# Attention on one core: the narrow matmuls of two key tiles gathered into one burst per pair of tiles

## The chip, the cores and the metric

The kernel runs on one core of a Trainium2 chip. The metric is the device time of one execution in microseconds (us). The kernel before took 3467.74 us, the median of three runs (3467.65 to 3473.09).

## What is computed

The program runs two layers over x of 2 sequences x 2048 tokens x 512 features. The first layer (a state-space mixer and a feed-forward network, both conditioned) is not touched. The second layer is attention with 16 heads of width 32:

```python
h = _sln(hidden, w, ln_g, ln_b, Wg, bg, Wb, bb)
qkv = (h @ Wqkv.T + bqkv).reshape(B, N, num_heads, hd, 3)
...
energy = jnp.einsum('bhqd,bhkd->bhqk', q, k)
att = jax.nn.softmax(energy, axis=-1) / D ** 0.5
out = jnp.einsum('bhqk,bhkd->bhqd', att, v)
...
out = out @ Wp.T + bp
```

followed by the residual and a second conditioned layer norm. The change lies wholly in the three middle lines: scores, softmax, weighted sum of the values.

## The kernel before

The attention stage works in **blocks**: one block is 512 queries of one sequence for a group of 4 heads. There are 32 blocks (4 head groups x 2 sequences x 4 query chunks). A block walks over 16 **tiles** of 128 keys (`kt` in the code). The work of one tile is:

- **Scores** (PE, `score`, L1554): 4 matmuls, one for each head, of 97 rows x 128 columns against 512 queries, into one of 3 PSUM banks in turn (banks 0 to 2). The 97th row adds minus the row maximum of each query.
- **Exponentials** (ACT, L1650): one pass over each score bank into `probs`, of which there are 8 tiles. The bank is free again when the pass is done; `score` waits for the pass of three scores ago (`exp_ready`, L1551).
- **Value matmuls** (PE, `weigh`, L1565): 4 matmuls in fp32, one for each head, each 32 columns wide, side by side in bank 6 (the trace shows each as 2 instructions, so 8 in a group). They come `AV_LAG` = 2 tiles after the scores of the tile.
- **Ones matmuls** (PE, `total`, L1575): 4 matmuls of the same narrow form with a matrix of ones, for the softmax denominators, into bank 7. They take the sum of the probabilities of two tiles (`pair`, added by POOL, L1711) and come at odd tiles, `SUM_LAG` = 5 tiles late.

The kernel subtracts the true row maximum, so it finds it one block ahead. For that PE makes the scores of the **following** block in the other orientation (`search`, L1540, 96 rows x 128 queries against 512 keys), into 3 PSUM banks of their own in turn (banks 3 to 5), and DVE reduces each to a column of maxima (`find`, L1673). A block has 64 searches, spread over its tiles by `SHARES` (L1402): 4 in tile 0, 5 in each of tiles 1 to 12, none in tiles 13 to 15. A search waits until DVE has read the bank of three searches ago:

```python
pe.wait_ge(max_read, MAXES * (NB * it + n) + max(j - 2, 0))
```

When the 64 maxima are there, DVE turns and negates them, SP copies them into the row of the queries of the next block, and DVE divides the block before by its denominators (L1681, L1685).

Each engine works through its own instructions in the order in which the program lists them. The order on PE is written out in `one` (L1589): per tile score 0, search, score 1, search, then the narrow matmuls, then search, score 2, search, score 3, search. `searches()` issues nothing once the share of the tile is used up. Blocks 0 and 31 stand by themselves; the others run in a loop of four blocks a turn (`blocks`, L1432), with the same order.

Of the kernel before, what the change touches and what calls it, by code (L numbers as in the profile page):

```python
# [1380 lines left out]
def attention_stage(nc, sb, sem, psum, a, wp, first, q_dram, k_dram, v_dram, att_dram):  # L1381
# [21 lines left out]
    AV_LAG, SUM_LAG = 2, 5  # L1403
# [28 lines left out]
    def blocks(engine, block):  # L1432

        block(0, 0, True, False)
        with engine.Fori(0, ITERS - 1) as it:
            for n in range(1, NB):
                block(it, n, False, False)
            block(it + 1, 0, False, False)
        for n in range(1, NB):
            block(ITERS - 1, n, False, n == NB - 1)  # L1440

    with nc.Block() as block:
# [86 lines left out]
        @block.tensor  # L1529
        def _(pe):  # L1530
            def search(it, n, j):

                kc, qt, h = j // (HG * TT), j // HG % TT, j % HG
                if j == 0:
                    pe.wait_ge(q_ld[n], (Q_LD + ROW_LD) * it + Q_LD)
                if j in (0, MAXES // 2):
                    pe.wait_ge(k_ld[n // PB][2 * j // MAXES], 48 * (it // PER_GROUP + 1))

                pe.wait_ge(max_read, MAXES * (NB * it + n) + max(j - 2, 0))
                nc.tensor.matmul(psum[:, MX + j % 3, :], queries[n][0:R, h, qt * P:(qt + 1) * P],  # L1540
                                 keys[n // PB][0:R, h, kc * CH:(kc + 1) * CH], start=True, stop=True).then_inc(max_ready, 1)

            def score(it, n, kt, h):

                if kt == 0 and h == 0:

                    pe.wait_ge(q_ld[n], (Q_LD + ROW_LD) * (it + 1))
                unit = UNITS * n + HG * kt + h

                if unit >= 3:  # L1550
                    pe.wait_ge(exp_ready, NB * UNITS * it + unit - 2)  # L1551
                elif not (n == 0 and isinstance(it, int)):
                    pe.wait_ge(exp_ready, NB * UNITS * it)
                nc.tensor.matmul(psum[:, SC + unit % 3, :], keys[n // PB][0:R + 1, h, kt * P:(kt + 1) * P], queries[n][0:R + 1, h, :],  # L1554
                                 start=True, stop=True).then_inc(sc_ready, 1)

            def weigh(it, n, kt):

                tile = NKT * (NB * it + n) + kt
                pe.wait_ge(exp_ready, HG * (tile + 1))  # L1560
                if kt == 0:
                    pe.wait_ge(o_copied, NB * it + n + 1)
                    pe.wait_ge(v_ld[n // PB], 16 * (it // PER_GROUP + 1))
                for h in range(HG):
                    mm = nc.tensor.matmul(psum[h * HD:(h + 1) * HD, OUT, :], values[n // PB][:, kt, h * HD:(h + 1) * HD], probs[kt % NPROB][:, h, :],  # L1565
                                          start=(kt == 0), stop=(kt == NKT - 1))
                mm.then_inc(av_ready, 1)

            def total(it, n, p):

                pe.wait_ge(pair_ready, PAIRS * (NB * it + n) + p + 1)
                if p == 0:
                    pe.wait_ge(den_copied, NB * it + n + 1)
                for h in range(HG):
                    mm = nc.tensor.matmul(psum[h * HD:(h + 1) * HD, DEN, :], ones[:, :], pair[p % 2][:, h, :],  # L1575
                                          start=(p == 0), stop=(p == PAIRS - 1))
                mm.then_inc(sums_ready, 1)

            def lagged(it, n, kt, lag):

                if kt >= lag:
                    return it, n, kt - lag
                return (it, n - 1, kt + NKT - lag) if n > 0 else (it - 1, NB - 1, kt + NKT - lag)

            def pair_of(it, n, kt):

                return it, n, kt // 2

            def one(it, n, first, last):  # L1589
                following = (it, n + 1) if n < NB - 1 else (it + 1, 0)  # L1590
                j = iter(() if last else range(MAXES))
                for kt in range(NKT):

                    share = [next(j, None) for _ in range(SHARES[kt])]

                    def searches():
                        if share and (at := share.pop(0)) is not None:
                            search(*following, at)

                    if first and kt == AV_LAG:  # L1600
                        pe.wait_ge(consts, 1)
                        pe.wait_ge(ones_ld, 16 * (B - 1))
                    score(it, n, kt, 0)
                    searches()
                    score(it, n, kt, 1)
                    searches()
                    if kt >= AV_LAG or not first:
                        weigh(*lagged(it, n, kt, AV_LAG))
                    if (kt - SUM_LAG) % 2 == 0 and (kt >= SUM_LAG or not first):
                        total(*pair_of(*lagged(it, n, kt, SUM_LAG)))  # L1610
                    searches()
                    score(it, n, kt, 2)
                    searches()
                    score(it, n, kt, 3)
                    searches()

            blocks(pe, one)
            for kt in range(NKT, NKT + AV_LAG):
                weigh(ITERS - 1, NB - 1, kt - AV_LAG)
            for kt in range(NKT + 1, NKT + SUM_LAG, 2):  # L1620
                total(ITERS - 1, NB - 1, (kt - SUM_LAG) // 2)
# [381 lines left out]
```

## Time and profile before

| | us |
|---|---|
| median of three runs | 3467.74 |
| time of the profiled execution | 3469.48 |
| its span, first to last instruction | 3467.7 |
| attention stage in the span, about | 1440 to 3305 |
| mean granted TensorE clock, share of full | 0.967 |

The span is the part of the execution from the first to the last recorded instruction. PE stands for the matmul engine and PEld for its weight loads; DVE, ACT, POOL and SP are the vector, scalar, GpSimd and sync engines. A time in brackets in a timeline row is the idle time of the engine before that row, with what ended it. In a timeline, instructions that follow each other without a gap are merged into one row with a count. PE's durations overlap: the start of the next matmul says how long one occupies the array, not its own duration.

### The profile page before, as it was taken

The numbers are of one execution on the slowest core, as the hardware profiler recorded it, in microseconds if no ns is written. First come the engines' busy times: TensorE is split into PE (matmuls) and PEld (weight loads), VectorE is DVE, ScalarE is ACT, GpSimd is POOL, SyncE is SP. The second block draws the span as 40 slices with busy tenths as digits, with TensorE's granted clock in tenths as the row PEclk, the third lists the DMA queues.
The fourth block names the chain that finished last, engine by engine and source line by source line (L and its number), as shares of the span: only waits on it lengthen the run. The fifth ranks groups of instructions, "written<-read, shape, count | busy, mean of one in ns | idle before, by whom it ended". The sixth has DMA issues, their size and how long they took to land. (4 is left out here: it accounts for less than half of the span.)

```text
span 3467.7 us, 52215 instructions
## 1 busy us (share of the span) xinstructions
PE 3200.3 (92%) x16326; PEld 1973.9 (57%) x16326; DVE 2216.4 (64%) x3513; ACT 1527.7 (44%) x2770; POOL 1566.3 (45%) x538
## 2 busy tenths in 40 slices
PE   4786999999997989899999999999999999999976
PEld 2675777787775767644444444444444444444354
DVE  7885222222214436478888788888787887888458
ACT  2222232322222322355555555555555555556632
POOL 2665211001111110166666666666666665666655
PEclk8887999999998999999999999999999999999988
DMA  6233100000002463511031201122101230100044
GB/s 245 77 110 115 49 22 4 23 24 24 25 13 103 167 191 131 157 27 26 14 74 32 56 14 25 32 56 62 26 13 26 62 74 14 26 13 7 4 162 147
DMA packets 119434, 214.40 MB, mean 62 GB/s; under 512 B 11719, under 2 KB 29147, under 8 KB 118794
## 3 DMA queue, kind: packets, MB, share of 16 engines
q1 hardware_dynamic: 119180, 211.20, 20.3%
q8 instruction: 136, 2.23, 0.3%
q14 instruction: 118, 0.97, 0.1%
HBM read 135.34 MB, written 75.53 MB: 61 GB/s over the span
## 5 line engine op out<-in xcount | busy, mean ns | idle before, releaser
L1711 POOL TENSOR_TENSOR pair<-probs 128x2048 f32<-128x2048 f32 x256 | 1173.3, 4583 | 739.4 <-ACT probs L1650 739.4
L1673 DVE TENSOR_REDUCE part_max<-psum 128x1 f32<-128x512 f32 x1984 | 1227.7, 682 | 334.9 <-PE psum L1540 334.4
L1650 ACT ACTIVATE probs<-psum 128x512 f32<-128x512 f32 x2048 | 1068.6, 602 | 764.5 <-PE psum L1554 763.9
L1540 PE MATMUL psum<-keys,queries 96*128 96x512 f32 x1984 | 833.6, 420 | 5.2 <-DMA queries<-q_parts 5.2
L1554 PE MATMUL psum<-queries,keys 97*128 97x512 f32 x2048 | 794.1, 409 | 40.4 <-ACT probs L1650 28.9
L1540 PEld LDWEIGHTS psum<-keys,queries 96*128 96x128 f32 x1984 | 375.1, 189 | 458.8 <-DVE part_max L1673 375.2
L1565 PE MATMUL psum<-probs,values 128*32 128x512 f32 x4096 | 547.0, 606 | 4.1 <-ACT o_sum L1632 2.9
L1554 PEld LDWEIGHTS psum<-queries,keys 97*128 97x128 f32 x2048 | 381.1, 190 | 245.0 <-ACT probs L1650 176.9
L980 DVE TENSOR_TENSOR h_lo<-w_stage,h_hi 128x512 fp32r<-128x512 f32 x128 | 96.7, 756 | 528.3 <-ACT h_hi L918 528.3
L911 ACT ACTIVATE w_stage<-psum,b_col 128x512 f32<-128x512 f32 x128 | 88.3, 690 | 510.0 <-PE psum L38 510.0
L1024 POOL TENSOR_TENSOR ffn_u_lo<-ffn_u,ffn_u_hi 128x512 fp32r<-128x512 f32 x32 | 41.2, 1287 | 553.9 <-DVE ffn_u_hi L970 553.9
L1575 PE MATMUL psum<-pair,att_ones 128*32 128x512 f32 x2048 | 266.6, 592 | 2.7 <-POOL pair L1711 2.7
L36 PE MATMUL psum<-ffn_u_hi,w_hi 128*128 128x512 f32 x512 | 204.0, 398 | 6.4 <-DVE b_parts L1006 6.4
L36 PE MATMUL psum<-w_hi,h_hi 128*128 128x512 f32 x512 | 203.4, 397 | 0.0
L38 PE MATMUL psum<-ffn_u_lo,w_hi 128*128 128x512 f32 x512 | 203.0, 396 | 0.0
L37 PE MATMUL psum<-ffn_u_hi,w_lo 128*128 128x512 f32 x512 | 202.9, 396 | 0.0
L37 PE MATMUL psum<-w_hi,h_lo 128*128 128x512 f32 x512 | 202.8, 396 | 0.0
L38 PE MATMUL psum<-w_lo,h_hi 128*128 128x512 f32 x512 | 202.2, 395 | 0.0
L1565 PEld LDWEIGHTS psum<-probs,values 128*32 128x32 f32 x4096 | 80.9, 108 | 139.7 <-issue 97.2
L1371 POOL TENSOR_TENSOR qkv_u_lo<-qkv_u,qkv_u_hi 128x512 fp32r<-128x512 f32 x32 | 41.2, 1288 | 263.7 <-DVE qkv_u_hi L1316 263.7
L1575 PEld LDWEIGHTS psum<-pair,att_ones 128*32 128x32 f32 x2048 | 66.5, 110 | 156.2 <-issue 150.4
L1681 DVE RECIPROCAL den<-den 128x512 f32<-128x512 f32 x32 | 106.9, 3341 | 48.4 <-ACT den L1637 48.4
(305 smaller groups left out, 3734.9 us busy)
## 6 DMA issues: line engine op xcount, KB each, us to landing
queries<-q_parts SPq DMA_DIRECT2D x96, 256.0 KB, 4.8
keys<-k_parts SPq DMA_DIRECT2D x42, 512.0 KB, 7.2
x<-in_x_dram SPq DMA_DIRECT2D x8, 1024.0 KB, 7.9
y<-in_x_dram SPq DMA_DIRECT2D x8, 1024.0 KB, 6.4
y_rows<-y SPq DMA_DIRECT2D x8, 1024.0 KB, 5.1
qkv_z<-z_rows SPq DMA_DIRECT2D x8, 1024.0 KB, 5.5
q_parts<-qk_hi SPq DMA_DIRECT2D x32, 256.0 KB, 2.0
q_parts<-qk_lo SPq DMA_DIRECT2D x32, 256.0 KB, 2.3
```

The lines of the kernel that those rows point to most:

```text
L36: nc.tensor.matmul(out, w_hi, x_hi, start=first, stop=False)
L37: nc.tensor.matmul(out, w_lo, x_hi, start=False, stop=False)
L38: return nc.tensor.matmul(out, w_hi, x_lo, start=False, stop=last)
L980: dve.tensor_tensor(h_lo[j % NH][:, :], g[j % 2], h_hi[j % NH][:, :].bitcast(F32), ALU.subtract).then_inc(glo_ready, 1)
L1540: nc.tensor.matmul(psum[:, MX + j % 3, :], queries[n][0:R, h, qt * P:(qt + 1) * P], keys[n // PB][0:R, h, kc * CH:(kc + 1) * CH], start=Tr ...
L1554: nc.tensor.matmul(psum[:, SC + unit % 3, :], keys[n // PB][0:R + 1, h, kt * P:(kt + 1) * P], queries[n][0:R + 1, h, :], start=True, stop= ...
L1565: mm = nc.tensor.matmul(psum[h * HD:(h + 1) * HD, OUT, :], values[n // PB][:, kt, h * HD:(h + 1) * HD], probs[kt % NPROB][:, h, :], start= ...
L1575: mm = nc.tensor.matmul(psum[h * HD:(h + 1) * HD, DEN, :], ones[:, :], pair[p % 2][:, h, :], start=(p == 0), stop=(p == PAIRS - 1))
L1650: act.activation(probs[kt % NPROB][:, h, :], psum[:, SC + unit % 3, :], ACT.Exp).then_inc(exp_ready, 1)
L1673: dve.tensor_reduce(part_max[:, at, kc:kc + 1], psum[:, MX + j % 3, :], AX.X, ALU.max).then_inc(max_read, 1)
L1681: dve.reciprocal(den[:, :], den[:, :]).then_inc(inverted, 1)
L1711: pool.tensor_tensor(pair[p % 2][:, :, :], probs[2 * p % NPROB][:, :, :], probs[(2 * p + 1) % NPROB][:, :, :], ALU.add).then_inc(pair_read ...
```

## The change

```diff
--- before.py
+++ after.py
@@ -1604,10 +1604,12 @@
                     searches()
                     score(it, n, kt, 1)
                     searches()
-                    if kt >= AV_LAG or not first:
-                        weigh(*lagged(it, n, kt, AV_LAG))
-                    if (kt - SUM_LAG) % 2 == 0 and (kt >= SUM_LAG or not first):
-                        total(*pair_of(*lagged(it, n, kt, SUM_LAG)))
+                    if kt % 2 == 1:
+                        for lag in (AV_LAG + 1, AV_LAG):
+                            if kt >= lag or not first:
+                                weigh(*lagged(it, n, kt, lag))
+                        if kt >= SUM_LAG or not first:
+                            total(*pair_of(*lagged(it, n, kt, SUM_LAG)))
                     searches()
                     score(it, n, kt, 2)
                     searches()
```

Value matmuls that stood in the even tile `kt` move to the odd tile `kt + 1`, ahead of the ones that stand there. They now come 3 tiles after their scores; those of odd tiles still come 2 after, and the ones matmuls stay where they were. No instruction is added or removed; the other engines keep their order and their waits.

Two places show it. The first is PE's order in block 0, tiles 6 and 7, both with five searches. Before, from the value matmuls of tile 4 (in the middle of tile 6) to the ones matmuls in the middle of tile 7:

```order
L1565 MATMUL psum<-probs4,values0 32x512 x4
L1540 MATMUL psum<-keys0,queries1 128x512
L1554 MATMUL psum<-queries0,keys0 128x512
L1540 MATMUL psum<-keys0,queries1 128x512
L1554 MATMUL psum<-queries0,keys0 128x512
L1540 MATMUL psum<-keys0,queries1 128x512
L1554 MATMUL psum<-queries0,keys0 128x512
L1540 MATMUL psum<-keys0,queries1 128x512
L1554 MATMUL psum<-queries0,keys0 128x512
L1540 MATMUL psum<-keys0,queries1 128x512
L1565 MATMUL psum<-probs5,values0 32x512 x4
L1575 MATMUL psum<-pair1,att_ones 32x512 x4
```

Now, over the same piece:

```order
L1540 MATMUL psum<-keys0,queries1 128x512 x2
L1554 MATMUL psum<-queries0,keys0 128x512
L1540 MATMUL psum<-keys0,queries1 128x512
L1554 MATMUL psum<-queries0,keys0 128x512
L1540 MATMUL psum<-keys0,queries1 128x512
L1554 MATMUL psum<-queries0,keys0 128x512
L1540 MATMUL psum<-keys0,queries1 128x512
L1554 MATMUL psum<-queries0,keys0 128x512
L1540 MATMUL psum<-keys0,queries1 128x512
L1565 MATMUL psum<-probs4,values0 32x512 x4
L1565 MATMUL psum<-probs5,values0 32x512 x4
L1575 MATMUL psum<-pair1,att_ones 32x512 x4
```

The value matmuls of tile 4 have gone down nine rows, to stand beside those of tile 5. Two searches meet where they stood, and 18 scores and searches (10 searches, 8 scores) now lie between two bursts.

The second place is PE's order in tiles 13 to 15 of a block, which hold no searches (names without buffer numbers; - before, + now):

```order
-L1565 MATMUL psum<-probs,values 32x512 x4
-L1575 MATMUL psum<-pair,att_ones 32x512 x4
-L1554 MATMUL psum<-queries,keys 128x512 x4
-L1565 MATMUL psum<-probs,values 32x512 x4
-L1554 MATMUL psum<-queries,keys 128x512 x4
-L1565 MATMUL psum<-probs,values 32x512 x4
+L1565 MATMUL psum<-probs,values 32x512 x8
+L1575 MATMUL psum<-pair,att_ones 32x512 x4
+L1554 MATMUL psum<-queries,keys 128x512 x8
+L1565 MATMUL psum<-probs,values 32x512 x8
 L1575 MATMUL psum<-pair,att_ones 32x512 x4
 L1554 MATMUL psum<-queries,keys 128x512 x2
```

Eight scores now run without a break, where four stood on each side of a group of value matmuls.

## Rows read from the trace of the kernel before

**Rows 1.** Page of the profile, part 1: busy us, share of the span, instructions.

```profile
PE 3200.3 (92%) x16326; PEld 1973.9 (57%) x16326; DVE 2216.4 (64%) x3513; ACT 1527.7 (44%) x2770; POOL 1566.3 (45%) x538
```

**Rows 2.** Windows: busy us (count) of PE, PEld, DVE, ACT, POOL; clock; DMA; GB/s.

```profile
1900.00:2300.00 400.00, 390.42 (x2196) 188.31 (x2196) 325.28 (x472) 234.47 (x454) 251.81 (x55) 1.00 0.16 37
3240.00:3300.00 60.00, 54.98 (x322) 18.19 (x314) 15.50 (x5) 39.84 (x77) 43.60 (x11) 1.00 0.03 10
```

**Rows 3.** Page, costliest groups: busy us, mean ns of one | idle before it, releaser.

```profile
L1673 DVE TENSOR_REDUCE part_max<-psum 128x1 f32<-128x512 f32 x1984 | 1227.7, 682 | 334.9 <-PE psum L1540 334.4
L1650 ACT ACTIVATE probs<-psum 128x512 f32<-128x512 f32 x2048 | 1068.6, 602 | 764.5 <-PE psum L1554 763.9
...
L1540 PEld LDWEIGHTS psum<-keys,queries 96*128 96x128 f32 x1984 | 375.1, 189 | 458.8 <-DVE part_max L1673 375.2
```

**Rows 4.** Timeline of PE, one tile pair with searches: start, duration (us), operation, count.

```profile
1920.63 1.04 PE L1575 MATMUL psum<-pair,att_ones 128*32 128x512 f32 x8
1921.60 0.50 PE L1540 MATMUL psum<-keys,queries 96*128 96x512 f32 x1
1921.94 0.40 PE L1554 MATMUL psum<-queries,keys 97*128 97x512 f32 x1
...
1923.60 0.40 PE L1540 MATMUL psum<-keys,queries 96*128 96x512 f32 x1
1923.93 1.07 PE L1565 MATMUL psum<-probs,values 128*32 128x512 f32 x8
1924.92 0.50 PE L1540 MATMUL psum<-keys,queries 96*128 96x512 f32 x1
...
1927.25 1.07 PE L1565 MATMUL psum<-probs,values 128*32 128x512 f32 x8
1928.13 1.04 PE L1575 MATMUL psum<-pair,att_ones 128*32 128x512 f32 x8
```

**Rows 5.** Timeline of DVE, the same tile pair.

```profile
1922.14 3.08 DVE L1673 TENSOR_REDUCE part_max<-psum 128x1 f32<-128x512 f32 x5 [1.10 <-PE psum L1540]
1925.46 3.08 DVE L1673 TENSOR_REDUCE part_max<-psum 128x1 f32<-128x512 f32 x5 [0.24 <-PE psum L1540]
```

**Rows 6.** Timeline of all engines: first and fifth search after a burst, and the maxima between.

```profile
1981.31 0.50 PE L1540 MATMUL psum<-keys,queries 96*128 96x512 f32 x1
...
1981.84 2.48 DVE L1673 TENSOR_REDUCE part_max<-psum 128x1 f32<-128x512 f32 x4 [1.08 <-PE psum L1540]
...
1983.29 0.40 PE L1540 MATMUL psum<-keys,queries 96*128 96x512 f32 x1
```

**Rows 7.** Timeline of all engines, tiles 13 and 14, which hold no searches.

```profile
1958.54 0.96 PE L1554 MATMUL psum<-queries,keys 97*128 97x512 f32 x3
1959.07 2.06 ACT L1650 ACTIVATE probs<-psum 128x512 f32<-128x512 f32 x4 [1.40 <-PE psum L1554]
...
1959.72 0.50 PE L1554 MATMUL psum<-queries,keys 97*128 97x512 f32 x1 [0.22 <-ACT probs L1650]
...
1960.15 1.07 PE L1565 MATMUL psum<-probs,values 128*32 128x512 f32 x8
```

**Rows 8.** Timeline of PE: the ones matmuls from tile 11 to tile 5 of the next block.

```profile
2010.25 1.04 PE L1575 MATMUL psum<-pair,att_ones 128*32 128x512 f32 x8
...
2017.27 1.04 PE L1575 MATMUL psum<-pair,att_ones 128*32 128x512 f32 x8
...
2023.36 1.04 PE L1575 MATMUL psum<-pair,att_ones 128*32 128x512 f32 x8
...
2030.15 1.04 PE L1575 MATMUL psum<-pair,att_ones 128*32 128x512 f32 x8
...
2037.76 1.04 PE L1575 MATMUL psum<-pair,att_ones 128*32 128x512 f32 x8
...
2045.23 1.04 PE L1575 MATMUL psum<-pair,att_ones 128*32 128x512 f32 x8
```

## The prediction

> **What bounds the kernel now.** I read four views in this order: the page's busy times, the attention stage by windows, the costliest groups, and the timelines of single tiles. The page gives PE 92% of the span [rows 1]. The change touches only the attention stage, and there PE is busy nearly all the time at a granted clock of 1.00, which is the 2.4 GHz level [rows 2]. A busy PE need not be what sets the pace, so I ask in the timeline which wait ends last.
>
> In tiles with searches PE does not pause. From one ones group to the next, at 1920.63 and 1928.13, lie 18 full-width matmuls (10 searches, 8 scores) and three narrow groups [rows 4]. The parts, from starts:
>
> - a score or search among its like: 1921.94 to 1923.60 is seven steps, 0.237 us each;
> - from the last search to a narrow group: 0.33 (1923.60 to 1923.93), so 0.09 more than that step;
> - a narrow group followed by another: 0.88 (1927.25 to 1928.13);
> - a narrow group followed by a search: 0.99 for a value group (1923.93 to 1924.92), 0.97 for the ones group (1920.63 to 1921.60), so about 0.1 more than 0.88;
> - from that search to the next score: 0.34, again 0.1 more than a step.
>
> So going into narrow matmuls and out again costs 0.09 + 0.10 + 0.10 = 0.29 us beside the work. A pair of tiles has two such bursts: 18 x 0.237 + 3 x 0.88 + 2 x 0.29 = 7.49, and the trace says 7.50.
>
> DVE is close behind. Five maxima take 3.08 us, one is 682 ns long, so they start (3.08 - 0.68) / 4 = 0.60 apart [rows 3, 5]. Ten need 6.0 of the 7.5 us. DVE idles 1.10 us after the burst of two groups and 0.24 after the single group [rows 5]. It never gets far behind, because a burst comes after every five searches and lets it catch up.
>
> What ties them is the ring of three search banks. After a burst at T (the first search, 1981.31) the first maximum starts at T + 0.53 (1981.84). The fifth search starts at 1983.29 = T + 1.98 [rows 6]. It needs the bank of the second, whose maximum ends at T + 0.53 + 0.60 + 0.68 = T + 1.81, and starts 0.17 later. So search k starts at no less than **T + 1.38 + 0.60 (k - 4)**. For k = 5 this is exactly where PE is anyway (0.34 + 7 x 0.237 = 2.00). Before the change every count starts anew after five searches. The weight loads of the searches already show 375.2 us idle that DVE ended, hidden under matmuls [rows 3].
>
> **The change, part by part.** It is only a move of value groups on PE; no DMA and no instruction of another queue moves.
>
> *Bursts saved.* One burst less in each of the 8 tile pairs of a block: -0.29 us a pair on PE.
>
> *Tiles with searches.* Now 10 searches stand between two bursts. By PE alone the tenth starts at 0.34 + 16 x 0.237 = T + 4.13. By the banks it starts at T + 1.38 + 6 x 0.60 = T + 4.98. The scores stand between the searches in PE's order, so they wait as well. The burst follows 0.33 later and lasts 0.88 + 0.88 + 0.97 = 2.73. The next T is at 4.98 + 0.33 + 2.73 = **8.04**, against 7.48: +0.56 us. Two value groups side by side are not in the rows; a value group ahead of the ones group is the nearest (0.88, taken), the value group ahead of a search the other end (0.99, kept for the range; nothing in the rows speaks for less than 0.88). During the burst DVE has two to three banks waiting, 1.3 us of work or so, then idles: 8.04 - 6.0 = 2.0 us a pair. Nothing gives that back, since only three searches can be ahead.
>
> Stretches from one ones group to the next, in a block (those of before in [rows 8]):
>
> - tiles 3 to 5, 5 to 7, 7 to 9, 9 to 11: four of ten searches, before 7.47 (2037.76 to 2045.23; 7.50 in rows 4), taken as 7.48. Now 8.04: 4 x 0.56 = +2.24.
> - tiles 1 to 3: before 7.61 (a short wait for the copy of the last sums stands in it, and goes, because the first value group now comes a tile later). Now 8.04: +0.43.
> - tiles 11 to 13: before 7.02. It has eight searches: the eighth at T + 3.78, two scores 0.48, then 0.33 + 2.73: 7.32. +0.30.
> - tiles 13 to 15: before 6.09, scores only. PE waits for ACT there: score 4 starts 1.18 after score 1, as the first exponential starts at + 0.53 and lasts 0.60; then 0.43 to the value group [rows 7]. Exponentials start (2.06 - 0.60) / 3 = 0.49 apart [rows 3, 7]. Now eight scores stand together, and score 8 needs exponential 5: 0.53 + 4 x 0.49 + 0.60 + 0.06 = 3.15. Then 0.43 + 2.73: 6.31. +0.22.
> - tiles 15 to 1 of the next block: before 6.79. Six searches and eight scores: banks allow search 6 at about T + 3.4 (first search at 0.8, ACT sets score 7 at 2.66 and score 8 at 3.15). Then 0.33 + 2.73: 6.47. -0.32.
>
> Sum 2.24 + 0.43 + 0.30 + 0.22 - 0.32 = +2.87 us a block. With 31 blocks that hold searches: +89.0. The last block has none, seven stretches x 0.22 = +1.5. Together **+90.5 us**. Costed at nothing: the row of maxima for the next block (SP's copy). The last maximum starts 0.53 + 7 x 0.60 = 4.7 after tile 11's burst, the next block's first score now at 7.32 + 6.31 + 0.6 = 14.2, so 9.5 us cover it; before it was about 5.0 against 13.7, 8.7 us. SP's reload of the values waits for the last value group of a block, tile 15's, which stays in its tile. ACT's `probs` are 8 tiles deep and the moved groups come 3 late instead of 2. The sum that POOL makes for a pair is wanted two pairs later as before. If one of these covers failed, it would be a wait once a block, not in every pair.
>
> The sum stands on the profiled execution, 3469.48, giving 3560.0; that is 1.7 above the median of the runs, so the median goes to **3558**.
>
> The Trainium skill, "TensorEngine Tiling (Array Packing)", section "Tiling Modes", says that changing the tiling mode drains the engine. Rows 4 agree, with 0.29 us for a change there and back. By this rule alone the change is a gain, the first rival below; the rule says nothing of the banks.
>
> **The rivals.**
>
> *PE stays the bound, faster.* Then only the saved bursts count: 8 x 0.29 x 32 = -74 us, 3394. For it: PE's 92%, DVE's 1.3 us idle in each pair. It needs the maxima at most (4.13 - 1.38) / 6 = 0.46 us apart; even to break even they would have to be 0.51. Against it: 0.60 in every row of five. A second way to it would be that the searches' wait lets scores pass, but PE keeps its order. Chance 0.06.
>
> *The two cancel.* Within 0.2%, 7 us, what a measurement of this kernel can tell from no change: needs a pitch near 0.51. Chance 0.02.
>
> *The forecast.* Slower by 90, between 57 and 124. If the hand-over after a maximum costs nothing (0.17 less): -0.85 us a block; if in addition the stretch 15 to 1 gains 0.2 more, -33 in all, 3525 with rounding. If two value groups take 0.99: 0.11 x 8 x 32 = +28; with 6 us more for maxima 0.61 apart, 3592. Chance 0.84.
>
> *DVE's own 0.68 sets the pitch,* not 0.60: the tenth search then starts 6 x 0.08 = 0.5 later, 5 stretches x 0.5 x 31 = +75 more, 3633. Against it: the merged rows of five. Chance 0.04.
>
> *The clock falls.* PE, now waiting some tenths of a us before each search, drops from 2.4 to 1.2 GHz at times. The 7.19 us of PE work in a pair would then take 14.4, 6.3 above 8.04; in one pair in ten (20 of 200) this is +130, 3690. Against it: the tiles without searches at 3240 to 3300 hold a wait in every tile, and the clock there is 1.00 [rows 2, 7]. Chance 0.04. The Trainium skill, "TensorE: Matmul & The Clock Gate", section "A second HAM failure mode: psum-queue depth-cycling", tells of such short idle gaps between matmul groups making the clock swing; by those windows this trace does not bear it out.
>
> **How the numbers follow.** The time is that of the forecast, 3558, its range 3525 to 3592, which holds 0.84 of the chance, less a little for terms I have not seen. Faster 0.06, same 0.02, slower 0.84 + 0.04 + 0.04 = 0.92.
>
> **What would show it.** In the profile after: ones groups 8.0 us apart in tiles 3 to 11 (7.2 if the rival holds); maxima in merged rows of about ten, 6.1 us long, then 2 us idle; PE idle before searches 6 to 10, released by DVE's maxima, some 0.1 to 0.2 us each; three narrow groups 0.88 apart; clock still 1.00 in the stage; tiles 13 to 15 at 6.3. The prediction is wrong if the tenth search stands near T + 4.1, if the pitch of the maxima moves off 0.60 when ten come in a row, or if PE finds another way to lose or save time inside the burst.

## The result, and the profile after

The changed kernel takes 3569.73 us (median of four runs, 3566.45 to 3574.98); the kernel before took 3468.75 in the runs beside it. The ratio is 1.0282, 95% interval 1.0269 to 1.0296: slower by about 100 us. The forecast was slower, 3558, in a range of 3525 to 3592.

The page after, part 1 and three of the costliest groups (busy us, mean ns of one | idle before it, releaser):

```profile
PE 3292.8 (92%) x16326; PEld 1959.2 (55%) x16326; DVE 2211.6 (62%) x3513; ACT 1566.1 (44%) x2770; POOL 1564.3 (44%) x538
...
L1675 DVE TENSOR_REDUCE part_max<-psum 128x1 f32<-128x512 f32 x1984 | 1208.3, 680 | 435.5 <-PE psum L1540 434.8
L1652 ACT ACTIVATE probs<-psum 128x512 f32<-128x512 f32 x2048 | 1107.2, 607 | 827.7 <-PE psum L1554 821.6
...
L1540 PEld LDWEIGHTS psum<-keys,queries 96*128 96x128 f32 x1984 | 373.0, 188 | 509.6 <-DVE part_max L1675 317.8
```

PE is as busy as before, 92% [rows 1], in a program 100 us longer, and one maximum of DVE (680 ns) and one exponential of ACT (607 ns) take what they took [rows 3]. None of these shares tells what happened. The weight loads of the searches idled 375.2 us until DVE before, 317.8 after: even this sum fell.

The timeline of PE over one ten-search stretch of the changed kernel does tell (start, duration; the row at 2012.11 holds the fifth and sixth search):

```profile
2009.16 1.04 PE L1575 MATMUL psum<-pair,att_ones 128*32 128x512 f32 x8
2010.13 0.50 PE L1540 MATMUL psum<-keys,queries 96*128 96x512 f32 x1
...
2012.11 1.00 PE L1540 MATMUL psum<-keys,queries 96*128 96x512 f32 x2
2012.94 0.40 PE L1554 MATMUL psum<-queries,keys 97*128 97x512 f32 x1
2013.20 0.50 PE L1540 MATMUL psum<-keys,queries 96*128 96x512 f32 x1
...
2014.40 0.50 PE L1540 MATMUL psum<-keys,queries 96*128 96x512 f32 x1
...
2014.99 0.50 PE L1540 MATMUL psum<-keys,queries 96*128 96x512 f32 x1
2015.43 1.92 PE L1565 MATMUL psum<-probs,values 128*32 128x512 f32 x16
2017.17 1.04 PE L1575 MATMUL psum<-pair,att_ones 128*32 128x512 f32 x8
2018.14 0.50 PE L1540 MATMUL psum<-keys,queries 96*128 96x512 f32 x1
```

From one ones group (2009.16) to the next (2017.17) it is 8.01 us; before it was 7.50 [rows 4]. From the sixth search on, each stands 0.60 after the last (2013.20, then 2014.40 two later, 2014.99), not two steps of 0.237, and each has a row of 0.50 us, like the first search behind a burst, against 0.40 in the flow. PE's rows show no pause before them; the wait stands in the rows of their weight loads (PEld), which idle 0.30 us until DVE before each of the last four searches:

```profile
2014.40 0.19 PEld L1540 LDWEIGHTS psum<-keys,queries 96*128 96x128 f32 x1 [0.30 <-DVE part_max L1675]
...
2014.99 0.19 PEld L1540 LDWEIGHTS psum<-keys,queries 96*128 96x128 f32 x1 [0.30 <-DVE part_max L1675]
```

The two value groups take 1.74 together, 0.87 each. The row of the tenth search is at T + 4.86, the value groups at T + 5.30; the forecast had 5.31.

DVE over the same time (start, duration, count, idle before):

```profile
2010.66 6.07 DVE L1675 TENSOR_REDUCE part_max<-psum 128x1 f32<-128x512 f32 x10 [1.94 <-PE psum L1540]
2018.67 6.07 DVE L1675 TENSOR_REDUCE part_max<-psum 128x1 f32<-128x512 f32 x10 [1.94 <-PE psum L1540]
```

Ten maxima run without a gap in 6.07 us, (6.07 - 0.68) / 9 = 0.60 apart, and then DVE idles 1.94 us while the burst runs; before it was twice 3.08 with 1.10 and 0.24 idle [rows 5].

Where the 100 us lie, from the starts of all 256 ones groups in both traces, summed over the 31 blocks with searches (the first ones group of block 0 stands in tile 5, so tiles 1 to 5 count 30 blocks):

```
stretch (tile to tile)     before   after   difference over the blocks
3-5, 5-7, 7-9, 9-11          7.48    8.01   +65.3 (four stretches)
1-3                          7.61    8.01   +10.3
11-13                        7.01    7.28    +8.4
13-15                        6.08    6.29   +19.1, of it 12.7 in 8 blocks at 7.8 to 7.9
15-1 of the next             6.79    6.52    -4.9
last block                                   +2.8, of it 1.5 in tiles 1 to 3, 8.25 instead of 6.68
sum                                        +100.9
```

The before and after columns are medians; the parts are rounded. In the last block's tiles 1 to 3 of the changed kernel the clock fell too (granted 0.59 over the value groups); 1.5 is its excess over the 6.78 that stand there in runs where it did not fall. One row holds something that was not in the forecast's main line: eight blocks spend 7.8 to 7.9 us in tiles 13 to 15 instead of 6.29. Two such stretches in PE's timeline, the slow one:

```profile
2049.45 0.96 PE L1554 MATMUL psum<-queries,keys 97*128 97x512 f32 x3
2050.64 2.45 PE L1554 MATMUL psum<-queries,keys 97*128 97x512 f32 x5 [0.23 <-ACT probs L1652]
2053.02 3.60 PE L1565 MATMUL psum<-probs,values 128*32 128x512 f32 x16
2056.37 1.13 PE L1575 MATMUL psum<-pair,att_ones 128*32 128x512 f32 x8
```

and a usual one:

```profile
2172.06 1.04 PE L1575 MATMUL psum<-pair,att_ones 128*32 128x512 f32 x8
2173.03 0.96 PE L1554 MATMUL psum<-queries,keys 97*128 97x512 f32 x3
2174.21 2.46 PE L1554 MATMUL psum<-queries,keys 97*128 97x512 f32 x5 [0.23 <-ACT probs L1652]
2176.60 1.92 PE L1565 MATMUL psum<-probs,values 128*32 128x512 f32 x16
2178.34 1.04 PE L1575 MATMUL psum<-pair,att_ones 128*32 128x512 f32 x8
```

In both the eight scores go alike. The two value groups, 1.74 us in the usual one, take 3.35 in the other. The windows (busy us of PE, PEld, DVE, ACT, POOL, then the granted clock):

```profile
2001.14:2009.16 8.02, 7.93 (x47) 3.69 (x43) 6.07 (x10) 4.85 (x9) 4.57 (x1) 1.00 0.00 0
2049.45:2053.02 3.57, 3.34 (x12) 1.42 (x8) 3.44 (x2) 3.03 (x7) 1.87 (x1) 1.00 0.02 2
2053.02:2056.37 3.35, 3.35 (x17) 0.81 (x20) 3.23 (x1) 1.00 (x3) 2.67 (x1) 0.52 0.02 5
```

During the scores the clock is 1.00, during the value groups 0.52, that is 1.2 GHz almost throughout. In the ten-search stretch, the first row, it is 1.00.

The clock falls at one more kind of place, and does so before the change too: where the loop of four blocks turns, PE pauses 1 to 2 us in the stretch from tile 15 to tile 1. The kernel before, PE's timeline and a window:

```profile
2430.17 0.73 PE L1554 MATMUL psum<-queries,keys 97*128 97x512 f32 x2
2433.07 0.49 PE L1554 MATMUL psum<-queries,keys 97*128 97x512 f32 x1 [2.17 <-issue]
...
2434.06:2437.47 3.41, 3.41 (x13) 1.08 (x12) 1.51 (x3) 0.88 (x2) 2.35 (x1) 0.50 0.78 187
```

Of the six turns, two fall to 0.50 behind the pause in this trace and take 10.5 to 10.7 us; the other four take 8.6 to 9.0. In the changed kernel it is two of six as well (10.5 and 10.8), so the 100 us hold nothing of it. In the runs below it is two to six of six, and this moves totals by several us.

### The profile page after: what moved, and what is told of

The parts are those of the page before. It is cut to its first block and busy times, and to the rows that moved or that the text cites. A ratio compares the mean times of both kernels' runs of the same rounds, so it can differ in the third digit from the quotient of the medians.

```text
span 3567.9 us, 52215 instructions
## 1 busy us (share of the span) xinstructions
PE 3292.8 (92%) x16326; PEld 1959.2 (55%) x16326; DVE 2211.6 (62%) x3513; ACT 1566.1 (44%) x2770; POOL 1564.3 (44%) x538
## 5 line engine op out<-in xcount | busy, mean ns | idle before, releaser
L1675 DVE TENSOR_REDUCE part_max<-psum 128x1 f32<-128x512 f32 x1984 | 1208.3, 680 | 435.5 <-PE psum L1540 434.8
L1652 ACT ACTIVATE probs<-psum 128x512 f32<-128x512 f32 x2048 | 1107.2, 607 | 827.7 <-PE psum L1554 821.6
L1540 PE MATMUL psum<-keys,queries 96*128 96x512 f32 x1984 | 895.3, 454 | 23.0 <-DMA queries<-q_parts 5.4
L1554 PE MATMUL psum<-queries,keys 97*128 97x512 f32 x2048 | 816.5, 414 | 31.2 <-ACT probs L1652 25.8
L1540 PEld LDWEIGHTS psum<-keys,queries 96*128 96x128 f32 x1984 | 373.0, 188 | 509.6 <-DVE part_max L1675 317.8
L1565 PE MATMUL psum<-probs,values 128*32 128x512 f32 x4096 | 507.8, 614 | 0.0
L1565 PEld LDWEIGHTS psum<-probs,values 128*32 128x32 f32 x4096 | 108.6, 111 | 230.0 <-ACT probs L1652 116.8
```

The lines of the kernel that those rows point to most:

```text
L1652: act.activation(probs[kt % NPROB][:, h, :], psum[:, SC + unit % 3, :], ACT.Exp).then_inc(exp_ready, 1)
L1675: dve.tensor_reduce(part_max[:, at, kc:kc + 1], psum[:, MX + j % 3, :], AX.X, ALU.max).then_inc(max_read, 1)
```

## The experiments

The theory, here "bank theory": the loss comes from the ring of three search banks together with maxima 0.60 us apart, which hold the sixth and later searches of a stretch. The gain of the saved bursts is real and smaller. Rivals: the longer burst itself, the value groups coming a tile later, the clock.

**Make DVE faster, in both kernels.** The edit, in `find`:

```diff
-dve.tensor_reduce(part_max[:, at, kc:kc + 1], psum[:, MX + j % 3, :], AX.X, ALU.max)
+dve.tensor_reduce(part_max[:, at, kc:kc + 1], psum[:, MX + j % 3, 0:CH // 2], AX.X, ALU.max)
```

On the kernel before. 

> The kernel before, with each maximum taken over 256 of the 512 scores of its bank (it leaves out half of the keys in the row maxima). DVE's maxima should start about 0.35 us apart instead of 0.60. Bank theory: before the change PE sets the pace in tiles with searches and the fifth search is just not held, so nothing moves: ones groups 7.45 to 7.48 apart, 3465 to 3469 us. Rival (DVE already set the pace before): 7.2 or less apart and at least 40 us faster.

Measured: 3472.86 us, ratio 1.0007 (0.9996 to 1.0018), ones groups 7.48 apart. DVE did not set the pace before. The total lies 4 us over the expected range; in the trace the stretches with a loop turn hold 7 us more than before, and the clock fell at four of the six turns.

On the changed kernel. 

> The changed kernel, with each maximum over 256 of 512 scores (half of the keys left out of the row maxima). Bank theory: with maxima 0.35 apart the tenth search is no longer held, ones groups stand 7.19 apart in tiles 3 to 11, and the saved bursts show alone: about 3468 - 5 x 0.29 x 31 - tiles 11 to 1 0.5 x 31 = 3405 to 3415, some us more if the clock still falls in tiles 13 to 15. Rival (the loss comes from the burst itself, from the value groups coming later, or from the clock): it stays within 10 us of 3570.

Measured: 3425.08 us, ratio to before 0.9861 (0.9844 to 0.9879). PE's timeline of one stretch:

```profile
2018.42 0.39 PE L1540 MATMUL psum<-keys,queries 96*128 96x512 f32 x1
2018.74 1.92 PE L1565 MATMUL psum<-probs,values 128*32 128x512 f32 x16
2020.48 1.04 PE L1575 MATMUL psum<-pair,att_ones 128*32 128x512 f32 x8
2021.45 0.50 PE L1540 MATMUL psum<-keys,queries 96*128 96x512 f32 x1
...
2027.60 1.04 PE L1575 MATMUL psum<-pair,att_ones 128*32 128x512 f32 x8
```

The ones groups stand 7.12 apart, the tenth search is followed at once by the burst. The weight loads of the searches, from the page of this kernel:

```profile
L1540 PEld LDWEIGHTS psum<-keys,queries 96*128 96x128 f32 x1984 | 378.6, 191 | 234.9 <-issue 156.2
```

The wait for DVE is no longer what ends most of their idle time. So the same edit that gives nothing before gives 145 us after: the loss hangs on the pace of DVE's maxima, and the change without it would be a gain of 44 us. A saved burst is worth 7.48 - 7.13 = 0.35 us, rather more than the 0.29 forecast. The rest to the expected 3405 to 3415 is mostly the clock: eight blocks stand at 7.9 in tiles 13 to 15 in this kernel too, as does one stretch of the last block, and it fell at five of the six loop turns. One maximum takes 424 ns. Where DVE has the next bank waiting, maxima start 0.34 to 0.36 apart, as expected; that is so for about a fifth of them, and most of the others start 0.46 to 0.48 apart, as PE now sends the searches.

**An eighth less.** The same edit with 448 columns, on the changed kernel. 

> The changed kernel with each maximum over 448 of the 512 scores (an eighth of the keys left out of the row maxima). From 680 ns at 512 and 424 ns at 256 one maximum should take 0.62, and they should start 0.54 apart. Bank theory: tenth search at 0.53 + 6 x 0.54 + 0.62 + 0.17 = T + 4.56, ones groups 7.5 to 7.6 apart in tiles 3 to 11, tiles 11 to 13 about 7.0, all other stretches as in the changed kernel: 3570 - 31 x 2.7 = 3486. Rival (a threshold, or something beside DVE holds the searches): 7.1 or 8.0 apart.

Measured: 3485.90 us, ratio 1.0049 (1.0033 to 1.0064). Ones groups 7.54 apart, tiles 11 to 13 at 6.95, the others as in the changed kernel. DVE's timeline:

```profile
1991.35 5.41 DVE L1675 TENSOR_REDUCE part_max<-psum 128x1 f32<-128x448 f32 x10 [2.15 <-PE psum L1540]
```

Ten in 5.41 us with 616 ns for one: 0.53 apart. 512, 448 and 256 columns give 8.01, 7.54 and 7.13: no threshold in the middle, the stretch follows the pitch until PE's own order holds it.

**One search bank less.** The changed kernel:

```diff
-pe.wait_ge(max_read, MAXES * (NB * it + n) + max(j - 2, 0))
+pe.wait_ge(max_read, MAXES * (NB * it + n) + max(j - 1, 0))
-nc.tensor.matmul(psum[:, MX + j % 3, :], ...
+nc.tensor.matmul(psum[:, MX + j % 2, :], ...
-dve.tensor_reduce(..., psum[:, MX + j % 3, :], AX.X, ALU.max)
+dve.tensor_reduce(..., psum[:, MX + j % 2, :], AX.X, ALU.max)
```

> The changed kernel with two search banks instead of three, the score banks untouched. Bank theory: a search waits for the maximum of two before, which starts at the earliest 0.17 + 0.68 after that one, so maxima are some 0.64 to 0.66 apart and the tenth search stands near T + 5.8: ones groups 8.85 apart in tiles 3 to 11 (8.01 with three banks), tiles 13 to 15 unchanged at 6.29; 3570 + 31 x 5.3 = 3735. Rival (the ring is not what holds): below 3600.

Measured: 3754.19 us, ratio 1.0804 (1.0779 to 1.0829), ones groups 8.88 apart, tiles 13 to 15 at 6.29. DVE's timeline:

```profile
2090.96 6.43 DVE L1675 TENSOR_REDUCE part_max<-psum 128x1 f32<-128x512 f32 x10 [2.44 <-PE psum L1540]
```

Ten maxima now take 6.43, (6.43 - 0.68) / 9 = 0.64 apart. The ring sets the time, as expected. The total lies 19 us over the expected 3735: the clock fell in tiles 13 to 15 of six blocks and at all six loop turns, for which nothing had been put in.

**One search bank more, at the cost of a score bank.** Eight banks are all there are, so four search banks leave two for the scores; on the changed kernel and on the one before:

```diff
-SC, MX, OUT, DEN = 0, 3, 6, 7
+SC, MX, OUT, DEN = 0, 2, 6, 7
-... max(j - 2, 0))          MX + j % 3        unit - 2)       SC + unit % 3
+... max(j - 3, 0))          MX + j % 4        unit - 1)       SC + unit % 2
```

(Shortened: the wait and the bank of a search, then those of a score; DVE and ACT read the same banks.)

> The changed kernel with four search banks and two score banks instead of three and three. Bank theory: search k waits for the maximum of four before, so the tenth starts at T + 1.38 + 5 x 0.60 = 4.38 instead of 4.98, ones groups 7.4 to 7.5 apart in tiles 3 to 11 (8.01 in the changed kernel). Tiles 13 to 15 get slower with two score banks, 7.0 instead of 6.3. In all 3570 - 5 x 0.6 x 31 + 0.7 x 39 = about 3505. Rival (burst or lag): tiles 3 to 11 stay at 8.0, the whole at 3590 or more.

> Control for the run before: the kernel before with four search banks and two score banks. Bank theory: PE sets the pace in tiles with searches, so a fourth search bank gives nothing there, 7.47 apart; two score banks cost in tiles 13 to 15 only, about 0.3 to 0.5 a pair: 3475 to 3490. Rival (search banks already bound before): 7.3 or less apart in tiles 3 to 11.

Measured: 3662.67 us on the changed kernel (ratio 1.0554, 1.0534 to 1.0574) and 3626.41 on the one before (1.0442, 1.0423 to 1.0461). Both expectations of the totals miss. In tiles 3 to 11 the changed kernel goes from 8.01 to 7.68, less than expected; the control goes from 7.48 to 7.99. What I left out is that a ring of two scores binds in tiles with searches too. The control's timeline, scores and exponentials behind a burst:

```profile
2052.34 0.40 PE L1554 MATMUL psum<-queries,keys 97*128 97x512 f32 x1
...
2052.77 2.27 ACT L1650 ACTIVATE probs<-psum 128x512 f32<-128x512 f32 x4 [2.15 <-PE psum L1554]
2052.81 0.40 PE L1554 MATMUL psum<-queries,keys 97*128 97x512 f32 x1
...
2053.42 0.50 PE L1554 MATMUL psum<-queries,keys 97*128 97x512 f32 x1
```

The third score starts at 2053.42, when the first exponential (2052.77, 0.60 long) is over, and so it goes on in every stretch. In the changed kernel the wait for DVE is gone (0.8 us in all in its table of waits, against 317.8 with three banks) and the wait of the scores for ACT has taken its place (483.7). The pair of runs fits the bank theory but is no clean test of it, since two rings change at once; it does show that no bank can be spared for the searches. In the changed kernel with two score banks, tiles 13 to 15 lie over 8 us in 28 of 31 blocks, and in each of the 28 the granted clock fell to 1.2 GHz around the value groups.

**The rivals' own parts.** The value groups together, but the ones group on its own in even tiles:

```diff
                     if kt % 2 == 1:
                         for lag in (AV_LAG + 1, AV_LAG):
                             ...
-                        if kt >= SUM_LAG or not first:
-                            total(...)
+                    elif kt >= SUM_LAG or not first:
+                        total(...)
```

with `SUM_LAG` 4 instead of 5 (and the ones groups behind the last block a tile earlier to match). 

> The value groups of two tiles stand together in odd tiles as in the change, but the ones group stands alone in even tiles (four tiles late). Bank theory: five searches between bursts again, the longest burst is two groups as before, and the number of bursts is that of before, so ones groups 7.48 apart and 3460 to 3472 us. Rival (value groups of even tiles coming three tiles late, or two of them side by side, cost): over 3500.

Measured: 3469.99 us, ratio 1.0001 (0.9991 to 1.0010). A value burst of two groups (x16) and a ones group in turn, PE's timeline:

```profile
1996.30 1.92 PE L1565 MATMUL psum<-probs,values 128*32 128x512 f32 x16
...
2000.48 1.06 PE L1575 MATMUL psum<-pair,att_ones 128*32 128x512 f32 x8
...
2007.95 1.06 PE L1575 MATMUL psum<-pair,att_ones 128*32 128x512 f32 x8
```

7.47 apart, as before the change. Value groups side by side and a tile late cost nothing; what costs is ten searches in a row.

The price of a burst, from the other side: the kernel before with the ones group one score and two searches further down:

```diff
                         weigh(*lagged(it, n, kt, AV_LAG))
+                    searches()
+                    score(it, n, kt, 2)
+                    searches()
                     if (kt - SUM_LAG) % 2 == 0 and (kt >= SUM_LAG or not first):
                         total(*pair_of(*lagged(it, n, kt, SUM_LAG)))
-                    searches()
-                    score(it, n, kt, 2)
-                    searches()
                     score(it, n, kt, 3)
```

> The kernel before with the ones group moved away from the value group, behind the next search, score 2 and search, so that odd tiles hold two bursts of one group. It prices a burst: PE pays 0.29 more in each pair of tiles, ones groups 7.77 apart, 8 x 32 x 0.29 = 74 us more, 3542. Rival (going in and out of narrow matmuls is hidden or cheap while others wait): 3500 or less.

Measured: 3531.77 us, ratio 1.0179 (1.0163 to 1.0194), 7.80 apart in tiles 3 to 11: 0.33 for a burst more. The total is 10 us under the expected one, because tiles 11 to 13 and 13 to 15 went down, 7.01 to 6.87 and 6.08 to 5.93, where 0.29 more had been expected. That was a hint for the last run.

**The tail of the block as before.** The changed kernel, but tiles 14 and 15 with a value group each:

```diff
+                    if kt in (14, 15):
+                        weigh(*lagged(it, n, kt, AV_LAG))
-                    if kt % 2 == 1:
+                    elif kt % 2 == 1:
...
```

(The ones matmuls keep their place in every odd tile.)

> The changed kernel, but tiles 14 and 15 keep one value group each as before. Expected: tiles 13 to 15 take 6.08 again instead of 6.29, and the half clock that the changed kernel shows there in eight blocks (7.8 to 7.9 instead of 6.29) is gone: 3570 - 31 x 0.2 - 14 = 3550. Rival (the clock falls for PE's waits before the searches, anywhere): rows at half clock stay, in other tiles, and the time is 3560 or more.

Measured: 3560.83 us, ratio 1.0269 (1.0251 to 1.0287); the profiled execution has a span of 3553.5. Tiles 13 to 15 take 6.08 in every block, and none shows the half clock. The waits of the searches for DVE are as in the changed kernel (315.7 us). So the half clock in tiles 13 to 15 comes with eight scores in a row, not with the waits before the searches. The time of the runs moved by 9 us, not 20, and by its letter the rival holds as well: 3560 or more, and rows at half clock in other tiles. These rows are the loop turns, five of six at half clock against two in the changed kernel; the six turns take 5.9 us more than in the kernel before, in the changed kernel 0.3. They don't speak for the rival's cause: the kernel before falls there too, none falls in tiles 3 to 11, where the searches wait, and before each of the five falls PE pauses for 1.6 to 1.9 us. How many turns fall differs from kernel to kernel, with no rule that the runs show.

**The change where it gains only.** The kernel before, with the value group of tile 14 moved from tile 0 to tile 1:

```diff
-                    if kt >= AV_LAG or not first:
+                    if kt >= AV_LAG:
+                        weigh(*lagged(it, n, kt, AV_LAG))
+                    elif kt == 1 and not first:
+                        weigh(*lagged(it, n, kt, AV_LAG + 1))
                         weigh(*lagged(it, n, kt, AV_LAG))
```

> The kernel before, but with only the value group of tile 14 moved from tile 0 to tile 1 of the next block, where six searches lie between the bursts. Bank theory: this stretch is the one where the change gains, 6.52 instead of 6.79, with nothing lost elsewhere: 31 x 0.27 = 8 us faster than before, 3460. Rival (no stretch with more searches than five may lose its burst): same or slower than 3468.

Measured: 3466.50 us, ratio 0.9988 (0.9979 to 0.9997). PE's timeline of the stretch:

```profile
2022.59 1.04 PE L1575 MATMUL psum<-pair,att_ones 128*32 128x512 f32 x8
...
2027.04 0.40 PE L1540 MATMUL psum<-keys,queries 96*128 96x512 f32 x1
2027.37 1.92 PE L1565 MATMUL psum<-probs,values 128*32 128x512 f32 x16
2029.11 1.04 PE L1575 MATMUL psum<-pair,att_ones 128*32 128x512 f32 x8
```

6.52 instead of 6.79. So it is in 17 of the 31 stretches from tile 15 to tile 1; every fourth, seven in all, goes from 7.75 to 7.53, and the one into the last block, which has no searches, rises from 6.08 to 6.29. The six turns of the loop take 2.7 us more than before, with three at half clock instead of two; all other stretches are as before. The mechanism is as expected, the gain in the time is 4 us of the expected 8, with an interval that nearly touches none.

**The opposite of the change.** With it, in tiles 13 to 15 and the last block, the groups spread out:

```diff
+                    spread = kt >= 13 or (last and kt >= SUM_LAG - 1)
...
+                    if spread and kt % 2 == 0:
+                        score(it, n, kt, 2)
+                        weigh(*lagged(it, n, kt, AV_LAG))
+                        score(it, n, kt, 3)
+                        continue
...
+                    late = spread and (kt < 15 or last)
...
+                    if late:
+                        total(*pair_of(*lagged(it, n, kt, SUM_LAG)))
```

(`late` takes the ones group from its old place to the end of the tile.) 

> The opposite of the change where PE has no searches, and the change where it gains: the kernel before with the value group of tile 14 in tile 1 of the next block (as in the run on the edge alone), and in tiles 13 to 15 (and the last block) the three narrow groups of a pair spread out, two or three scores apart. By the same steps the burst is then short enough for three score banks to bridge: tiles 11 to 15 take 7.8 + 4.65 = 12.45 from ones group to ones group instead of 13.1, pairs of the last block 5.4 instead of 6.08, tiles 15 to 1 6.5 instead of 6.79, rest as before: 3468 - 31 x 0.95 - 5 = 3433. Rival (a burst more costs PE 0.29 and gains nothing, as in tiles with searches): slower than 3468.

Measured: 3447.46 us, ratio 0.9934 (0.9921 to 0.9947), the fastest of the kernels that take their maxima over all the keys. PE's timeline in tiles 14 and 15:

```profile
2014.83 1.07 PE L1575 MATMUL psum<-pair,att_ones 128*32 128x512 f32 x8
2015.83 0.97 PE L1554 MATMUL psum<-queries,keys 97*128 97x512 f32 x3
2016.73 1.06 PE L1565 MATMUL psum<-probs,values 128*32 128x512 f32 x8
2017.73 0.97 PE L1554 MATMUL psum<-queries,keys 97*128 97x512 f32 x3
2018.62 1.07 PE L1565 MATMUL psum<-probs,values 128*32 128x512 f32 x8
2019.51 1.04 PE L1575 MATMUL psum<-pair,att_ones 128*32 128x512 f32 x8
```

Two or three scores, one group, and no row waits for ACT. Tiles 11 to 15 take 7.79 + 4.66 = 12.45, pairs of the last block 5.44, tiles 15 to 1 6.52: each as expected. The whole is 14 us above the expected 3433. The six turns of the loop take 7.4 us more than before, with four at half clock instead of two; where the rest went is open.

## Why the prediction was right

By its own steps:

- *What bounds before.* PE, with DVE just behind. Halving DVE's work gave nothing (1.0007).
- *The formula for search k, ten-search stretches 8.04.* Measured 8.01. Two of the 0.03 are the value groups, 0.87 instead of 0.88. Inside the stretch two small misses cancel: the row of the tenth search starts at T + 4.86, not 4.98, and the burst follows 0.44 behind it, not 0.33. The idle time that was to stand before PE's searches, 0.1 to 0.2 us, stands before their weight loads, 0.30 us. The formula also gave the stretches with other pitches (7.54) and other rings (8.88).
- *Tiles 1 to 3, 11 to 13, 13 to 15, 15 to 1: 8.04, 7.32, 6.31, 6.47.* Measured 8.01, 7.28, 6.29, 6.52.
- *Bursts saved, 0.29.* Undersized: 0.35 (the changed kernel with half the maxima) and 0.33 (the split). It made no difference to the sum, since PE was not the bound after. The rival "PE stays the bound" had its condition right: with maxima that can start closer than 0.46 the change gains. Its gain of 74 us was too high (measured 44), although a burst is worth more than it said, because the tiles without searches lose on pairing and the clock falls in some of them.
- *The range.* Its 6 us for maxima 0.61 apart should be 9 by the forecast's own formula (6 x 0.01 in 5 stretches of 31 blocks); the result does not lean on it.
- *The sum, +90.5.* Without the half-clock stretches of the eight blocks and the last one the ones groups give 100.9 - 12.7 - 1.5 = 86.7. So the steps forecast some 4 us too much, and the clock, of which the sum had nothing, brought 14 us.
- *The clock.* This is the step that failed. The forecast put 0.04 on it, with PE's waits before the searches as the cause, and held against it that the tiles without searches kept 1.00 [rows 2, 7]. It fell in just those tiles, in eight of 31 blocks, once eight scores stood in a row instead of four. Tiles 3 to 11, where the searches wait, kept 1.00 in every block with searches, in this and in all other runs. The windows of rows 2 hold neither of the two loop turns at which the clock falls before the change. The Trainium skill, "TensorE: Matmul & The Clock Gate", section "A second HAM failure mode: psum-queue depth-cycling", tells of short idle gaps between matmul groups with which the clock swings. The trace agrees only in part: the eight scores hold one gap of 0.22 us, and in eight of 31 blocks the value groups behind them ran at 0.52; before the change tiles 13 to 15 held two such gaps, and no block fell. The question to ask was what the change does to each stretch of matmuls, not only where PE waits.
- *Chances.* Nothing in the runs speaks against the order of the cases.

Open: which blocks fall to half clock. The eight (0, 1, 9, 10, 12, 14, 15, 19) show no pattern that I could test; in the kernel with half maxima it was eight blocks again, of which one (15) is the same.

## What to carry to other kernels

An engine that waits on a ring of banks is held by how much of the consumer's work stands between two pauses, not by the consumer's share of busy time: count the requests between bursts, multiply by the consumer's pitch, and compare with what the producer needs for them. Bursts of other work are the consumer's time to catch up. Gathering them saves the switch but makes the run between them longer, so gather only where the run is short, and where another ring is starved by the burst (here ACT's, in the tiles without searches), spread them.

## What was not expected of the hardware

- Going from full-width matmuls to groups 32 columns wide and back cost 0.33 to 0.35 us, more than the 0.29 that the gaps at its edges add up to.
- Behind eight full-width matmuls spread over 3.6 us, the later ones 0.49 us apart and with one gap of 0.22 us, the clock stood at 1.2 GHz over the next 3.35 us (granted 0.52) in eight of 31 blocks; behind four it did in none. With two score banks, where PE pauses 0.45 us and twice 0.19 us in them, it was 28 of 31.
- Behind a single pause of PE of about 1 to 2 us, at the turn of the loop, the clock fell to 1.2 GHz (granted 0.50) in two of six cases before the change and in two to six of six in the other runs.
- A maximum over a PSUM bank takes 680 ns for 512 columns, 616 for 448 and 424 for 256. Where the next bank waits, the next maximum starts 0.60, 0.53 and 0.34 to 0.36 us after the last, so before the last one's row ends.
